# Small expert blocks set in pairs with whole ones, and each pair's weight pieces spread anew

## What is computed

```python
scores = softmax(xf @ gate_w.T + gate_b)            # 8 experts
top_w, top_idx = top_k(scores, 2)                   # two experts a token, weights normalised
h = silu((xf @ gw.T + gb) * (xf @ uw.T + ub))       # F = 816
acc = acc + w[:, None] * (h @ dw.T + db)            # for each expert
```

## Time and profile before

| | |
|---|---|
| median of 3 runs | 1090.44 us |
| the profiled execution's own time | 1092.87 us |
| its span in the profile | 1091.0 us |
| TensorE / VectorE / ScalarE / GpSimd busy | 94% / 77% / 75% / 67% of the span |
| expert stage, from block 0's first matmul | 514.8 us to the end |
| TensorE's mean granted clock | 0.975 of full |

### The profile page before, as it was taken

The page is one execution under the profiler, slowest core; times in us unless marked ns, Lnnn a source line. Parts: engine busy times, 40 slices in busy tenths (PEclk is TensorE's granted clock), DMA queues, the critical chain, the costliest instruction groups (busy, mean ns, idle before and its releaser), DMA issues.

```text
span 1091.0 us, 28705 instructions
## 1 busy us (share of the span) xinstructions
PE 1021.6 (94%) x8622; PEld 944.2 (87%) x8622; DVE 839.4 (77%) x1962; ACT 816.8 (75%) x1983; POOL 735.7 (67%) x1041
## 2 busy tenths in 40 slices
PE   4857999999999999989999999999999999999996
PEld 3645778888888888869999999999999999999996
DVE  6488566666666667666798899898898899887773
ACT  6555868787878787867788888888888788886664
POOL 3267656364646464533589888888888888887774
PEclk9898999999999999999999999999999999999788
DMA  9791112020202010414522222237324532366641
GB/s 313 225 313 47 50 36 73 34 67 34 67 34 67 34 43 34 169 35 146 177 57 32 39 39 39 38 92 217 76 39 100 135 68 38 96 201 205 207 146 41
DMA packets 61811, 106.41 MB, mean 98 GB/s; under 512 B 8960, under 2 KB 50688, under 8 KB 59584
## 3 DMA queue, kind: packets, MB, share of 16 engines
q1 hardware_dynamic: 47680, 86.04, 24.4%
q0 software_dynamic: 14080, 19.74, 9.6%
HBM read 128.55 MB, written 35.59 MB: 150 GB/s over the span
## 4 chain that ended last, share of the span: by engine, by line
PE 43%; POOL 20%; issue 13%; DMA 5%; ACT 3%; DVE 2%; POOLq 1%; SPq 0%; DVEq 0%; ACTq 0%
POOL ht L715 11%; PE bank L1485 10%; PE bank L1486 10%; PE bank L1487 10%; POOL dw_s L705 4%; PE bank L1586 4%; DMA out_dram<-ys,dest 4%; POOL out_dram L727 3%; PE bank L1576 2%; PE bank L1607 2%; PE bank L1614 2%; ACT sm L816 1%; PE bank L1623 1%; ACT pt L821 1%; DMA raw_gu<-in_gu_dram 1%
## 5 line engine op out<-in xcount | busy, mean ns | idle before, releaser
L1485 PE MATMUL bank<-xt_h,gu_s 128*128 128x256 f32 (+3 forms) x1014 | 291.3, 287 | 5.1 <-DVE hf L1367 3.0
L1486 PE MATMUL bank<-xt_l,gu_s 128*128 128x256 f32 (+3 forms) x1014 | 289.2, 285 | 0.0
L1487 PE MATMUL bank<-xt_h,gu_s 128*128 128x256 f32 (+3 forms) x1014 | 288.6, 285 | 0.0
L715 POOL TENSOR_TENSOR ht<-hf,ht 128x256 fp32r<-128x256 f32 (+3 forms) x266 | 230.4, 877 | 48.1 <-ACT ht L943 37.4
L1485 PEld LDWEIGHTS bank<-xt_h,gu_s 128*128 128x128 f32 (+1 forms) x1014 | 196.2, 193 | 5.5 <-DVE gu_s L1336 3.2
L1336 DVE TENSOR_TENSOR gu_s<-raw_gu,gu_s 128x512 fp32r<-128x512 f32 (+1 forms) x273 | 199.1, 751 | 2.3 <-ACT gu_s L950 2.0
L1487 PEld LDWEIGHTS bank<-xt_h,gu_s 128*128 128x128 f32 (+1 forms) x1014 | 195.9, 193 | 0.0
L1486 PEld LDWEIGHTS bank<-xt_l,gu_s 128*128 128x128 f32 (+1 forms) x1014 | 195.5, 193 | 0.0
L931 ACT ACTIVATE gs<-bank,bias 128x256 f32<-128x256 f32 (+1 forms) x234 | 105.5, 452 | 84.0 <-PE bank L1487 79.4
L727 POOL DMA_INDIRECT out_dram<-ys,dest x71 | 120.3, 1694 | 54.4 <-POOL ht L715 24.7
L816 ACT ACTIVATE sm<-sm,least 128x256 f32<-128x256 f32 x256 | 127.0, 501 | 36.7 <-DVE least L1164 36.6
(11 more groups left out here) (213 smaller groups left out, 2610.3 us busy)
## 6 DMA issues: line engine op xcount, KB each, us to landing
raw_gu<-in_gu_dram SPq DMA_DIRECT2D x39, 1648.0 KB
raw_dw<-in_dw_dram SPq DMA_DIRECT2D x39, 768.0 KB
xr<-xs_dram SPq DMA_DIRECT2D x32, 258.0 KB
xs_dram<-zrec SPq DMA_DIRECT2D x5, 1548.0 KB, 17.0
raw_dw<-in_dw_dram SPq DMA_DIRECT2D x78, 64.0 KB
xwin<-xt_dram SPq DMA_DIRECT2D x7, 640.0 KB, 4.1
xt_dram<-xt SPq DMA_DIRECT2D x8, 512.0 KB, 5.7
xres<-in_x_dram SPq DMA_DIRECT2D x8, 512.0 KB, 3.8
```

Source lines behind the costliest of these rows:

```text
L715: nc.gpsimd.tensor_tensor(low, hf[0:m, ring(c), 0:n], ht[0:m, p, 0, c, 0:n].bitcast(F32), ALU.subtract).then_inc(h_split, 1)
L1485: nc.tensor.matmul(dst, lhs[0], rhs[0], start=start, stop=False)
L1486: nc.tensor.matmul(dst, lhs[0], rhs[1], start=False, stop=False)
L1487: return nc.tensor.matmul(dst, lhs[1], rhs[0], start=False, stop=stop)
```

## The change

Block numbers 0 to 26 are whole as before. From 27 on, small and whole blocks alternate: 27, 29, 31, 33, 35, 37 are small, 28 to 36 even are whole, and 38 is small. So every whole block from 26 on lies in buffer set 0, with small ones in set 1 up to 37. A small block behind a whole one is called `early`, a block behind a small one `late`. `new` becomes 1 for 16 blocks: 0 to 3, 16 to 18, 24, 25, and then 27, 29, 31, 33, 35, 36, 37 (38 has the expert of 36). The loops with a register run to block 23 or 24 instead of 29 or 30; the rest is written out. The pieces go as follows:

- Of an early block VectorE makes all 7 high pieces (ScalarE none), in the tail of the block two before it; its 7 low pieces come one behind each product of the whole block in front of it.
- Of a late block the 4 high pieces of VectorE come inside the small block in front of it, each behind a product and ahead of its low piece; its other 3 low pieces come at the end of that block. Nothing stands between a whole block's last product and the small block's first.
- In an early block the low part of the down weights of the block in front comes at chunk 3 instead of 1 on VectorE, and at chunks 2 to 4 instead of 0 to 2 on GpSimd; ScalarE copies those down weights at chunks 1 and 2 instead of between the blocks.

Apart from this, SyncE issues `load_gu(2, 0)` before it waits for the end of the dense stage and stores the last output group, instead of after.

The diff, without the counts of semaphores and the row offsets that follow from the new order:

```diff
+NE = 26
+SMALLS = [*range(NE + 1, NB, 2), NB - 1]
+WHOLES = [b for b in range(NB) if b not in SMALLS]
...
+        def late(b):
+            return isinstance(b, int) and b - 1 in SMALLS
+        def early(b):
+            return isinstance(b, int) and b in SMALLS and not late(b)
...
@@ sync
+            load_gu(2, 0)
             wait_dense_done(sp)
             store_out(NG - 1)
-            load_gu(2, 0)
             load_rows_of(2, 0)
...
-            with sp.Fori(0, (NF - 4) // 2) as i:
+            with sp.Fori(0, (NE - 4) // 2) as i:
                 load_block(i * 2 + 3, 1)
                 load_block(i * 2 + 4, 0)
-            for b in range(NF - 1, NB):
+            for b in range(NE - 1, NB):
...
@@ gpsimd body
                     h_low(b, p, c)
-                    if c < FCH - DV and (not isinstance(b, int) or b >= 1):
-                        dw_low(b - 1, 1 - p, DV + c)
+                    at = 2 if early(b) else 0
+                    if at <= c < at + FCH - DV and (not isinstance(b, int) or b >= 1):
+                        dw_low(b - 1, 1 - p, DV + c - at)
...
@@ scalar body
+                    if c in (1, 2) and early(b):
+                        dw_high(b - 1, 1 - p, (c - 1,))
-                if more and (not isinstance(b, int) or b >= 1):
+                if more and (not isinstance(b, int) or b >= 1) and not early(b + 1):
                     for c in range(FCH - GA, FCH):
                         gu_high(b + 1, 1 - p, c)
                     dw_high(b, p)
...
@@ vector route_blocks: one comparison over all blocks, one over the pairs' small blocks, one for the last
...
@@ vector body
                     up_times_gate(b, p, c)
-                    if more and c < FCH - GA:
+                    if late(b + 1) and c < FCH - GA:
+                        gu_high(b + 1, 1 - p, c)
+                    if c < FCH - GA or early(b + 1):
                         gu_low(b + 1, 1 - p, c)
-                    if c == 1:
+                    if c == (3 if early(b) else 1):
                         dw_low(b - 1, 1 - p)
...
-                if not isinstance(b, int) or b < NB - 2:
-                    for c in range(FCH - GA):
+                if not isinstance(b, int) or b < NB - 2 and not late(b + 2):
+                    for c in range(FCH if early(b + 2) else FCH - GA):
                         gu_high(b + 2, p, c)
-                for c in range(FCH - GA, FCH):
-                    gu_low(b + 1, 1 - p, c)
+                if not early(b + 1):
+                    for c in range(FCH - GA, FCH):
+                        gu_low(b + 1, 1 - p, c)
```

More of the change, by code:

```diff
@@ L33 @@
 SLOTS = NF * BT + NS * P
+NE = 26
+SMALLS = [*range(NE + 1, NB, 2), NB - 1]
+WHOLES = [b for b in range(NB) if b not in SMALLS]
+ROW_OF = {b: n * BT for n, b in enumerate(WHOLES)} | {b: NF * BT + n * P for n, b in enumerate(SMALLS)}
+assert len(SMALLS) == NS and WHOLES[0:NE + 1] == [*range(NE + 1)]
 REC = D + 2
@@ L347, in blocks_of, with high_count, high_count_act @@
             body(1, 1)
-            with eng.Fori(0, (NF - 4) // 2) as i:
+            with eng.Fori(0, (NE - 4) // 2) as i:
                 body(i * 2 + 2, 0)
                 body(i * 2 + 3, 1)
-            for b in range(NF - 2, NB):
+            for b in range(NE - 2, NB):
                 body(b, b % 2)
         def tiles_of(b):
-            return 1 if isinstance(b, int) and b >= NF else 2
+            return 1 if isinstance(b, int) and b in SMALLS else 2
+        def late(b):
+            return isinstance(b, int) and b - 1 in SMALLS
+        def early(b):
+            return isinstance(b, int) and b in SMALLS and not late(b)
+        def high_count(b, c):
+            return (FCH - GA) * b + (GA * sum(early(n) for n in range(b)) if isinstance(b, int) else 0) + (c + 1)
+        def high_count_act(b, c):
+            return GA * b - (GA * sum(early(n) for n in range(b)) if isinstance(b, int) else 0) + (c + 1 - (FCH - GA))
         def sent_by(b, p):
@@ L744, in _ @@
                 body(b, b % 2)
-            with pool.Fori(0, (NF - 4) // 2) as i:
+            with pool.Fori(0, (NE - 4) // 2) as i:
                 body(i * 2 + 3, 1)
                 body(i * 2 + 4, 0)
-            for b in range(NF - 1, NB - 1):
+            for b in range(NE - 1, NB - 1):
                 body(b, b % 2)
@@ L955, in dw_high @@
                     act.wait_ge(y_full, b - 1)
-                for cs in (slice(0, DV * D), slice(DV * D, DWW)):
+                for half in halves:
+                    cs = slice(DV * D, DWW) if half else slice(0, DV * D)
                     nc.scalar.activation(dw_s[p][:, 0, cs], raw_dw[:, p, cs], ACT.Copy).then_inc(dw_hi, 1)
@@ L1114, in route_blocks @@
             def route_blocks():
-                for at, end, ends in ((0, NF, r8[3]), (NF, NB, r8[10])):
-                    wide = [P, end - at, E]
-                    link(nc.vector.tensor_tensor(rb[:, at:end, :], spread(cst[:, C_BLK + at:C_BLK + end], wide), across(ends[:, :], wide), ALU.is_ge))
+                pairs = slice(NE + 1, NB)
+                for at, ends in ((slice(0, NB), r8[3]), (pairs, r8[10]), (slice(NB - 1, NB), r8[10])):
+                    count = (at.stop - at.start) // (2 if at is pairs else 1)
+                    wide = [P, count, E]
+                    ask = cst[:, C_BLK + at.start:C_BLK + at.stop]
+                    to = rb[:, at, :]
+                    if at is pairs:
+                        ask = ask.rearrange("p (n o) -> p n o", o=2)[:, :, 0]
+                        to = to.rearrange("p (n o) e -> p n o e", o=2)[:, :, 0, :]
+                    link(nc.vector.tensor_tensor(to, spread(ask, wide), across(ends[:, :], wide), ALU.is_ge))
                 link(nc.vector.tensor_reduce(rbs[:, :], rb[:, :, :], AX.X, ALU.add))
@@ L1470, in _ @@
             body(3, 1)
-            with dve.Fori(0, (NF - 6) // 2) as i:
+            with dve.Fori(0, (NE - 6) // 2) as i:
                 body(i * 2 + 4, 0)
                 body(i * 2 + 5, 1)
-            for b in range(NF - 2, NB - 1):
+            for b in range(NE - 2, NB - 1):
                 body(b, b % 2)
```

15 lines of the change are left out of this document (8 added, 7 removed).

## The result

The changed kernel takes 1126.3 us (median of 4 runs, 1122.04 to 1129.37) against 1090.37 us for the kernel before (4 runs): ratio 1.0313, interval 1.0269 to 1.0358 (the medians alone give 1.033). It is slower by 36 us, where 12 us less was forecast.

A forecast was written before the change was run, and what follows sets the result against it. TensorE was taken to bound the whole blocks, with 17.7 us lost over blocks 27 to 37. 17.7 - 9.1 (stalls) + 3.3 (early load) = 11.9 us off 1092.87: 1081.0, or 1078.5 against the median; range 1071 to 1091.

The forecast's parts named there:

- First term: TensorE's own work over blocks 27 to 37: same blocks in another order, 142.3 us again, nothing won or lost.
- Second: Weight loads in the pairs: VectorE may wait 1 to 2 us, cost on the path 0, up to 1.
- Third: VectorE's work per pair of whole and small block: about 24.6 of 25.75 us, so it fits, barely.
- The rival built on it: VectorE bounds the pair at 28.4 us, pairs can take 29.0, only 3.3 us remains: 1087 to 1090; chance 0.05.
- Fourth: Small block behind a whole one: down waits 0.8 to 1.8 us for dw_low, 0.3 to 0.5 for GpSimd; 9.1 in all.
- Fifth: Clock in the pairs: stalls of about 1.3 us bring no fall; a fall would cost 6.8 us each.
- falls in nearly every pair: Rival: clock falls at the whole block's down, waiting for dw_low, 6.8 us a time; 1096 to 1102; chance 0.12.
- Its counterweight: Argument against that rival: a fall gives GpSimd time to catch up, so the next stall should be short.
- Sixth: Blocks 0 and 1: load_gu(2, 0) leaves 2.4 us earlier, gaining 3.3 us, bounds 0 and 3.7.
- Nothing else: Rest of the kernel: routing comparison, fewer loop turns and written-out blocks cost nothing; tail behind T0(38) kept at 23.2 us.

The follow-up runs named there:

- g3_all: Changed kernel, early blocks: use_meta behind the last h_low, VectorE's dw_low at chunk 2, rows issued ahead of down weights; 1096.98 us, 1.0049 of the kernel before.
- h2_all_up: g3_all with, in early blocks, ScalarE's halves at chunks 0 and 1, GpSimd's pieces at 1 to 3, VectorE's dw_low at 1; 1087.68 us, 0.9952 of before.
- g1: Changed kernel, early blocks: use_meta behind the last h_low and VectorE's dw_low at chunk 2 instead of 3; 1099.97 us, 1.0075 of the kernel before.
- f1: Changed kernel with use_meta of an early block moved to its end, behind the last h_low; 1105.33 us, 1.011 of the kernel before.
- f2: Changed kernel with GpSimd's three down pieces at chunks 0 to 2 in early blocks too, ahead of the scatter wait; 1106.65 us, 1.0111 of the kernel before.
- g4: Changed kernel's block order and early load, but every piece where the kernel before has it; 1108.62 us, 1.0166 of the kernel before.
- h1: g3_all with, in early blocks, ScalarE's halves at chunks 0 and 1 and GpSimd's pieces at 1 to 3; 1093.18 us, 1.0001 of the kernel before.

## Why the prediction was wrong

**First term (TensorE's work): right.** A whole block behind a small one takes 11.9 us wherever nothing holds it, in every kernel with the new order; 12.18 was priced. The stretch of the changed kernel, less its idle time (23.1) and half of its 61.4 us at half clock, is 140.4; 142.3 was priced. (A slip without weight: the second stretch at half clock in the earlier trace rows is 13.6 us long, not 13.4.)

**Second (loads): right for the changed kernel, with a hole beside it.** raw_gu is late by up to 2.7 us for VectorE in the changed kernel and by 4.5 in g3_all, and TensorE does not see it; in h2_all_up it sees one of 4.4, by 1.0 us. But the term followed only the weights through SyncE's queue to their reader. The rows of the same block stand behind `load_dw` in that queue, which waits for GpSimd's last piece. TensorE waited for them 1.0 to 1.2 us in each of four pairs of the changed kernel, 4.2 in all (0.4 to 2.4 and 6.7 in g1), and the longest falls of the clock came behind these waits. The sum had this wait at nothing.

**Third (VectorE fits): right.** 129.5 us busy of 155.5 in h2_all_up. The rival built on it, that VectorE bounds every pair at 28.4 to 29.0, is not borne out: four of five pairs are under its 28.4, at a mean of 27.8. VectorE held TensorE up only behind the one late load.

**Fourth (the small block behind a whole one, 9.1 us): this step failed.** The place was right, and the part that it was made of came out near: product 3 at T0 + 8.6 (7.1 to 8.1 forecast), dw_low done at T0 + 11.8 (9.6 to 10.6), half a us because product 3 was late and half because the piece took 1.74 us and not the 1.22 of the earlier trace rows. What it took to be small was GpSimd's third piece, "a further 0.3 to 0.5". I had walked GpSimd's queue past h_low 4 and not past `use_meta` at chunk 2, although a moved step must be followed past every instruction that it is moved behind. In the kernel before nothing urgent stood behind that wait, and no row of mine showed it. It measured 17.1 us of GpSimd's waiting in the changed kernel and 12.6 of TensorE's in the stretch, and f1 and f2 price it at 20 us with the clock that it brings down. With it gone, the stall of dw_low alone is 7.2 us over four blocks in f1, 1.8 each, the upper end of the 0.8 to 1.8 given for it; that this is near the 1.75 a pair of the whole term is partly luck, since two small blocks had none and the late rows, which the term did not hold, made another 5.8.

**Fifth (no clock falls): wrong, and about as large.** The forecast let no idle time under 1.5 us halve the clock. In f1, where only the foreseen stalls and the rows are left, the mean clock is still 0.89, which costs 0.11 x 173.4 = 19 us, most of it beside the waits for the rows; in g4 idle times of 0.92 did it. The rival "falls in nearly every pair" had the sign and, for blocks 27, 29 and 37, the place, the down of the whole block, but mostly the wrong wait there (dw_low, 5.7 us in three of the changed kernel's blocks, against 12.6 for GpSimd's pieces in five), and nothing of the rows, behind which the clock fell in the other three; at 0.12 it was too low. Its 6.8 us a time is not what was measured either: the clock cost 3.4 to 8.5 us in each of six small blocks, 30.7 in all. Its counterweight, that a fall gives the others time to catch up, held in block 33 (1.0 us of waiting for the pieces was left) and not in block 35 (3.0), where GpSimd waited 4.7 us for the landing.

**Sixth (the early load): right in the trace**, 2.9 of 3.3 us, and within a measurement's uncertainty by itself.

**"Nothing else": wrong by some 2 us or more.** T0(2) to T0(27) takes 368.5 us instead of 365.0, and 366.5 to 370.7 in the other kernels with the new order. Of the 3.5 us, 2.2 lie in block 26, whose pieces are already those of the pairs: it takes 16.7 us in place of 14.5 (16.6 in h2). The other 1.3 lie in block 17, a whole block that takes no longer than before in f1, so they are not clearly the change's. No run is without it.

**The sum.** It had 142.3 + 9.1 = 151.4 us for the stretch, and 194.2 were measured. The 42.8 between them are 30.7 of clock and 14.0 of idle time beyond the 9.1, less 1.9 of TensorE's work. With the wait passed, rows first and the pieces back at chunks 1 to 3 (h2) it is 155.5. The 8.8 us of idle time in it are near the 9.1, but by luck: they are waits for GpSimd's pieces (7.0) and for VectorE's product (1.4), not for dw_low. And the whole of h2 is 5 us faster than before, where the forecast was 12. The shift of the down weights by one or two chunks, which the change makes along with it, pays nothing in any of these runs: with h1 and h2, which take steps of it back, the ratio fell clear of noise, with g1 within it.

## What to carry to other kernels

When a step is moved in a queue, list every instruction between its old and new place and ask of each wait there how late it can end, above all those for a DMA's landing: a wait that cost nothing because nothing urgent stood behind it will cost its full length to the first urgent thing put there. Give a stall's price with the clock at half behind it until a row of the same place shows the contrary. And when a change has several parts, each with a reason, undo them one at a time: here the new order lost with the old places of the pieces (g4), lost more with those of the changed kernel, and with the down pieces put back came out with no clear gain over the early load alone. Follow every reader of a queue too: the rows stood in the same queue as the weights, and the sum had no price for their wait.

## What the runs showed of the hardware

A scatter that is issued just ahead of a load of weights can take long to land. In block 31 of the changed kernel the first 128 rows, issued at 982.39, landed 3.8 us later, and the second, issued at 984.30, 9.1 us later; the load of the gate and up weights left at 984.64, and the DMA engines were 71% busy from 986.7 to 993.5. Between 550 and 860 us the median is 3.9 us. In the other small blocks behind a whole one, up to 35, the second took 8.4 to 10.3. In block 37, beside which no new weights are loaded, it took 3.6. That it is the load which delays the scatter is likely from this, but no run changed it alone.

The length of an idle time does not settle whether the clock falls. In g4_order_only 0.92 us in block 31 was followed by 13.6 us at 0.50; the same 0.92 us, at the same place and also ended by VectorE's product, was followed by full clock in block 37:

```profile
1069.42 0.30 PE L1521 MATMUL bank<-xt_h,gu_s 128*128 128x128 f32 x1 [0.92 <-DVE hf L1400]
```

In h2_all_up 1.03 us in block 32, and another 0.35 behind it, was followed by full clock too. What else decides isn't shown here.

The same work has different prices. VectorE's 128x1024 low part took 1.74 us in block 31 of the changed kernel, where GpSimd worked through all of it, and 1.22 in the earlier trace rows; GpSimd's 128x256 piece took 0.76 to 1.17 in that block. The Trainium skill (GPSIMD Engine Reference, section 1) says that the two engines share their interfaces to SBUF, with contention. The trace agrees in part: eight of the ten low parts from 905 to 1085 us took 1.74 to 1.77, and two took 1.21 though GpSimd was at work then too, so working side by side is not all that decides.
